# A patch-embedding tower on one core: early pair loads, earlier routing of the first groups, another opening, and the positions' squares folded into their table

## Time and profile before

| | us |
|---|---|
| timed runs (3) | 3396.25 to 3401.76, median 3399.97 |
| the profiled execution | 3385.79 |
| its span | 3383.9 |
| PE busy | 2483.1 (73%) |
| DVE busy | 2187.2 (65%) |
| ACT busy | 1658.6 (49%) |
| POOL busy | 2434.6 (72%) |

### The profile page before, as it was taken

How to read it: one execution, slowest core, us unless ns; L and a number is a source line. 1 busy time by engine, 2 the same in 40 slices (tenths; PEclk the granted TensorE clock), 3 DMA queues, 4 the chain that set the end, 5 groups by cost and what they waited for, 6 DMA issues and landing times. The chain is left out here.

```text
span 3383.9 us, 63281 instructions
## 1 busy us (share of the span) xinstructions
PE 2483.1 (73%) x14081; PEld 1880.2 (56%) x14082; DVE 2187.2 (65%) x7770; ACT 1658.6 (49%) x4362; POOL 2434.6 (72%) x2518
## 2 busy tenths in 40 slices
PE   5999995788777757666766377787787787777773
PEld 4877774454444434333433166676676676666663
DVE  5999997688876767767765444444444444577775
ACT  5988886556554545545543033333333333333332
POOL 4777772077777777777777777777777777777776
PEclk8999998567665676766665579878878878777886
DMA  8877872133333333333333154444444444699996
GB/s 304 285 262 264 268 266 102 35 98 105 104 104 95 101 96 96 100 96 99 98 97 96 63 135 128 128 126 114 112 113 112 111 112 113 212 303 302 303 303 214
DMA packets 401951, 522.41 MB, mean 154 GB/s; under 512 B 65661, under 2 KB 329555, under 8 KB 390579
## 3 DMA queue, kind: packets, MB, share of 16 engines
q1 hardware_dynamic: 318610, 373.60, 37.2%
q0 software_dynamic: 83232, 147.75, 12.9%
HBM read 257.02 MB, written 264.08 MB: 154 GB/s over the span
## 5 line engine op out<-in xcount | busy, mean ns | idle before, releaser
L1109 POOL DMA_INDIRECT ytk<-yo,idxy x1080 | 1055.8, 978 | 329.4 <-issue 324.2
L1100 POOL DMA_INDIRECT xed<-xr,idxs x1014 | 998.3, 985 | 392.0 <-issue 308.1
L1520 ACT ACTIVATE yo<-wide,gi 128x128 f32<-128x128 f32 x1080 | 307.8, 368 | 865.1 <-DMA ytk<-yo,idxy 836.5
L1372 PE MATMUL wide<-wdt,hT 64*128 x2160 | 376.0, 324 | 184.1 <-DVE hT L1877 181.1
L1868 DVE SCALAR_TENSOR_TENSOR ae<-the,bank 128x256 f32<-128x256 f32 x270 | 113.5, 420 | 604.1 <-ACT the L1511 590.9
L1354 PE MATMUL bank<-wgu,xeT 128*128 x2160 | 370.1, 325 | 140.8 <-ACT xeT L1505 138.1
L1372 PEld LDWEIGHTS wide<-wdt,hT 64*128 64x128 f32 x2160 | 316.9, 222 | 235.2 <-issue 232.1
L1354 PEld LDWEIGHTS bank<-wgu,xeT 128*128 128x128 f32 x2160 | 330.8, 234 | 182.2 <-issue 181.6
L594 POOL TENSOR_TENSOR weff<-w,gam 128x384 f32<-128x384 f32 x338 | 268.8, 830 | 10.1 <-DMA tokb<-in_tokb 8.7
L1282 PE MATMUL wide<-xn,e 128*128 128x128 f32 (+3 forms) x1024 | 274.2, 391 | 1.6 <-ACT e L1442 1.6
L1290 PE MATMUL wide<-ident,xr 128*128 128x128 f32 x169 | 44.6, 414 | 250.4 <-DVE xr L1613 250.4
(11 more groups left out here) (334 smaller groups left out, 5060.1 us busy)
## 6 DMA issues: line engine op xcount, KB each, us to landing
xin<-xed SPq DMA_DIRECT2D x1080, 74.0 KB
ytk<-zeros SPq DMA_DIRECT2D x42, 1536.0 KB, 9.6
yg<-ytk SPq DMA_DIRECT2D x42, 1536.0 KB, 7.9
xs<-in_xcol SPq DMA_DIRECT2D x42, 1280.0 KB, 6.7
ytk<-yo,idxy POOLq DMA_INDIRECT x1080
xed<-xr,idxs POOLq DMA_INDIRECT x1014
H<-in_ximg SPq DMA_DIRECT2D x4, 2704.0 KB, 22.1
h1d<-H SPq DMA_DIRECT2D x42, 256.0 KB, 9.5
```

The costliest lines, as they stand in the source:

```text
L1100: p.indirect_dma_start(xed[:, :], bass.IndirectOffsetOnAxis(ap=idxs[:, slot, j, k:k + 1], axis=0), xr[:, slot, j, :], None).then_inc(scat[ ...
L1109: p.indirect_dma_start(ytk[:, :], bass.IndirectOffsetOnAxis(ap=idxy[:, slot, j:j + 1], axis=0), yo[:, slot % ES, j, :], None)\
L1372: last = pe.matmul(eO[slot % 2][:, j * D:(j + 1) * D], hT[:, slot % 2, j, :], wdt[:, bass.ds(e, 1), :].rearrange("p o f -> p (o f)"), star ...
L1520: last = a.activation(yo[:, slot % ES, j, :], eO[slot % 2][:, j * D:(j + 1) * D], ACT.Copy, scale=gi[:, slot, j, 0:1])
```

## The change

It has four parts.

- `h1s` and the semaphores of its loads belong to the whole kernel. POOL clears it in the opening; SP loads the first two pairs at the end of the first stage, as soon as all h1 stores have landed, and the second stage doesn't load them or wait for the memset.
- `step_of` gives the first groups other steps: first halves at 3, 5, 6, 8 (before: 4, 6, 7, 9), second halves of the first three at 4, 6, 8 (before: 6, 7, 9). From the first half of group 4 and the second half of group 3 on, all is as before. SP's store of h4 has lag 2 instead of 3.
- In the opening ACT copies the row terms ahead of the second quarter of the images, not the fourth, and TensorE does `conv_x` of group 0 ahead of the positions' squares.
- The positions' squares are in the table itself: `post` becomes `sum_d(p^2 + 2 p) / D - 2 p`, and `xT` becomes x + 1. As a normalised x sums to 0 over d, the product is |p|^2 - 2 x.p. The splitting, three small DMAs, and the two bf16 products per group go; the squares are summed by two float32 products over all 128 partitions, and DVE combines them at the end of `statistics`. ACT's copy to `xT` is Identity with a bias of ones, where it was Copy.

```diff
+FIRST_HALF = {0: 3, 1: 5, 2: 6, 3: 8}
+SECOND_HALF = {0: 4, 1: 6, 2: 8}
+def step_of(g, lag, late):
+    if lag == 0:
+        return FIRST_HALF.get(g, place_of(g, late))
+    if lag == 1:
+        return SECOND_HALF.get(g, place_of(g + 1, late))
+    return place_of(g + lag, late)
...
+            elif isinstance(i, int):
+                for g in range(r_first, r_stop):
+                    if step_of(g, lag, late) == period * i + u:
+                        fn(g, g % 4, g // 4)
             elif third != 1:
-                g = 4 * i + (c - lag)
-                if not isinstance(g, int) or r_first <= g < r_stop:
-                    fn(g, (c - lag) % 4, i + (c - lag) // 4)
+                fn(4 * i + (c - lag), (c - lag) % 4, i + (c - lag) // 4)
...
+def load_pair(sp, h1d, h1s, h1_in, g, slot):
+    src = h1d[bass.ds(2 * g, 2), :, :].rearrange("b t d -> t b d")
+    sp.dma_start(h1s[:, slot, 0:4:2, :], src[0:HALF[0]]).then_inc(h1_in[slot], 16)
+    sp.dma_start(h1s[0:HALF[1], slot, 1:4:2, :], src[HALF[0]:T]).then_inc(h1_in[slot], 16)
...
-        def store_squares(sp):
...
+            g.memset(c["h1s"][:, :, :, :], 0.0).then_inc(s_zero, 1)
...
-        def split_squares(g):
...
+            v.wait_ge(s_psq, 3)
+            v.scalar_tensor_tensor(post[:, :], wide[1][:, 0:NN], 1.0 / D, post2[:, :], ALU.mult, ALU.subtract).then_inc(s_post, 1)
...
-                if i == 3:
+                if i == 1:
                     a.wait_ge(s_gb, 1)
...
-            a.activation(post[:, :], post[:, :], ACT.Copy, scale=-2.0).then_inc(s_psq, 1)
+            a.activation(post2[:, :], post[:, :], ACT.Copy, scale=2.0).then_inc(s_psq, 1)
...
-            pe.matmul(wide[1][0:1, 0:NN], ones[:, 0:1], possq[:, :], start=True, stop=True).then_inc(s_psq, 1)
+            pe.matmul(wide[1][:, 0:NN], ones[:, :], possq[:, :], start=True, stop=False)
+            pe.matmul(wide[1][:, 0:NN], ones[:, :], post2[:, :], start=False, stop=True).then_inc(s_psq, 1)
...
-                store_squares(sp)
...
-                sp.wait_ge(yt_zero, 16 * GA)
                 sp.wait_ge(h1_out[0], 16 * (-(-GA // 2)))
                 sp.wait_ge(h1_out[1], 16 * (GA // 2))
+                for g in range(2):
+                    load_pair(sp, h1d, c["h1s"], c["h1_in"], g, g)
+                sp.wait_ge(yt_zero, 16 * GA)
...
-                    pe.wait_ge(s_ps3, 48)
-                    nj = tiles_of(g)
-                    for j in range(0, nj, 2):
-                        m = min(2, nj - j)
-                        for i in range(j, j + m):
-                            pe.matmul(psD[:, i * NN:(i + 1) * NN], xT[:, i, :], post[:, :], start=(i == j), stop=False)
-                        last = pe.matmul(psD[:, j * NN:(j + m) * NN], onesb[0:3, :],
-                                         psq3[:, :].unsqueeze(1).to_broadcast([3, m, NN]), start=False, stop=True)
+                    pe.wait_ge(s_post, 1)
+                    for j in range(tiles_of(g)):
+                        last = pe.matmul(psD[:, j * NN:(j + 1) * NN], xT[:, j, :], post[:, :], start=True, stop=True)
...
-                position_squares(pe)
                 conv_x(0, 0, 0)
+                position_squares(pe)
...
-                    a.activation(xT[:, 0:nj, :].rearrange("p j d -> p (j d)"), psT[:, 0:nj * D], ACT.Copy).then_inc(xT_ready, 1)
+                    a.activation(xT[:, 0:nj, :].rearrange("p j d -> p (j d)"), psT[:, 0:nj * D], ACT.Identity,
+                                 bias=ones[:, 0:1]).then_inc(xT_ready, 1)
...
-            p.memset(h1s[:, :, :, :], 0.0).then_inc(n["s_h1"], 1)
...
-            sp.wait_ge(n["s_h1"], 1)
...
-            load_h1(0, 0, 0)
-            load_h1(1, 1, 0)
...
-                ('r', 3, halves(store_h4))], 0, GR)
+                ('r', 2, halves(store_h4))], 0, GR)
```

More of the change, by code:

```diff
@@ L202, in build @@
         mur = sb("mur", [128, B, 2, 2])
+        h1s = sb("h1s", [128, 2, 4, D])
+        h1_in = [sem(f"h1_in{i}") for i in range(2)]
         front(nc, io, sb, bank, wide, dict(
             ident=ident, identb=identb, ones=ones, onesb=onesb, before=before, beforeb=beforeb,
-            eps_ln=eps_ln, tenth=tenth, wq=wq, fscale=fscale, mur=mur), h1d, gbd, ytk)
+            eps_ln=eps_ln, tenth=tenth, wq=wq, fscale=fscale, mur=mur, h1s=h1s, h1_in=h1_in), h1d, gbd, ytk)
         back(nc, io, sb, sem, bank, wide, dict(
             ident=ident, identb=identb, ones=ones, onesb=onesb, before=before, beforeb=beforeb,
-            wq=wq, fscale=fscale, mur=mur, eps_ln=eps_ln), h1d, h3d, h4d, xed, ytk, out)
+            wq=wq, fscale=fscale, mur=mur, eps_ln=eps_ln, h1s=h1s, h1_in=h1_in), h1d, h3d, h4d, xed, ytk, out)
+def load_pair(sp, h1d, h1s, h1_in, g, slot):
+    src = h1d[bass.ds(2 * g, 2), :, :].rearrange("b t d -> t b d")
+    sp.dma_start(h1s[:, slot, 0:4:2, :], src[0:HALF[0]]).then_inc(h1_in[slot], 16)
+    sp.dma_start(h1s[0:HALF[1], slot, 1:4:2, :], src[HALF[0]:T]).then_inc(h1_in[slot], 16)
 def front(nc, io, sb0, bank, wide, c, h1d, gbd, ytk):
@@ L233, in front @@
         possq = sb("possq", [128, NN])
-        psqr = sb("psqr", [1, NN])
-        psq_parts = sb("psq_parts", [1, 3, NN], BF16)
-        psq3 = sb("psq3", [3, NN], BF16)
+        post2 = sb("post2", [128, NN])
         valt = sb("valt", [128, NN])
@@ L292, in front @@
         s_gpart = sem("s_gpart")
-        s_pq = sem("s_pq")
         s_const = sem("s_const")
@@ L305, in front @@
         s_psq = sem("s_psq")
-        s_psp = sem("s_psp")
-        s_ps3 = sem("s_ps3")
+        s_post = sem("s_post")
         s_v2 = sem("s_v2")
@@ L333, in store_rows @@
             sp.wait_ge(s_gbo, 96)
-        def store_squares(sp):
-            sp.wait_ge(s_psp, 5)
-            for k in range(3):
-                sp.dma_start(psq3[k:k + 1, :], psq_parts[:, k, :]).then_inc(s_ps3, 16)
         def constants(g):
@@ L608, in _ @@
                 split_rows(p)
-                split_squares(p)
                 fold(1, 1, 0)
@@ L676, in _ @@
                 mixed_values(pe)
+                conv_x(0, 0, 0)
                 position_squares(pe)
-                conv_x(0, 0, 0)
                 turn_moments(pe)
@@ L757, in _ @@
                 squares(a)
-                a.wait_ge(s_psq, 3)
-                a.activation(psqr[:, :], wide[1][0:1, 0:NN], ACT.Copy).then_inc(s_pq, 1)
                 a.wait_ge(s_mstd, 3)
@@ L879, in _ @@
                 v.wait_ge(s_mrT, 1)
-                v.wait_ge(s_zero, 2)
+                v.wait_ge(s_zero, 3)
                 mur = c["mur"]
@@ L968, in back @@
     uptob = sb("uptob", [128, 128], BF16)
-    h1s = sb_early("h1s", [128, 2, 4, D])
+    h1s, h1_in = c["h1s"], c["h1_in"]
     mrs = sb_early("mrs", [128, 2, 8])
@@ L1030, in back @@
     n = {}
-    for name in ("s_wt", "s_ws", "s_zr", "s_c", "upto_r", "s_c2", "s_h1",
+    for name in ("s_wt", "s_ws", "s_zr", "s_c", "upto_r", "s_c2",
                  "mrs_r", "xq_r", "q_r", "xqb_r", "qt_done", "xqT_r", "ffn_done", "h2_r", "bnc",
@@ L1041, in back @@
         n[name] = sem(name)
-    h1_in = [sem(f"h1_in{i}") for i in range(2)]
     h3_out = [sem(f"h3_out{i}") for i in range(2)]
@@ L1120, in load_h1 @@
                 after(sp, n["h2_r"], g - 1)
-                src = h1d[bass.ds(2 * g, 2), :, :].rearrange("b t d -> t b d")
-                sp.dma_start(h1s[:, slot, 0:4:2, :], src[0:HALF[0]]).then_inc(h1_in[slot], 16)
-                sp.dma_start(h1s[0:HALF[1], slot, 1:4:2, :], src[HALF[0]:T]).then_inc(h1_in[slot], 16)
+                load_pair(sp, h1d, h1s, h1_in, g, slot)
             def store_h3(g, slot, rnd):
```

2 lines of the change are left out of this document (1 added, 1 removed).

## The result

The kernel after took 3379.94 us (median of 6, 3377.11 to 3382.69), the kernel before on the same chip 3398.56 (6 runs): ratio 0.9939 (0.9929 to 0.9950), 18.6 us less. A copy of it, timed again on a second chip, took 3366.05 (5 runs) against 3384.50 (21): 0.9947 (0.9933 to 0.9960), 18.4 us less.

The account below looks back on a forecast made before the run. POOL's unbroken indirect DMAs from the first scatter on were taken to bound the end, DVE the first stage. Crossing -5.5, opening -4.5, squares -1.0 and routing -12.3 sum to -23.3: 3400.0 to 3376.7, so 3377 us, range 3360 to 3393.

Parts of the forecast that it names:

- rival C: The opening's stores land no sooner, or ACT starts late after the crossing: 3382 us; chance 0.14.
- The crossing: Between first and second stage: early loads let ACT start with the others at 581.5, -5.5 us, bounds 0 and -5.6.
- The opening: Start of the kernel: rows split sooner, conv_x(0) before the squares, conv_gb(0) near 49; -4.5 us, between 0 and -5.1.
- The squares: First stage: two bf16 matmuls fewer per group, gaining only in filling and draining; -1.0 us, bounds 0 and -31.
- Rival B: TensorE sets the pace of the first stage: a further -30 us, 3347; chance 0.08.
- The routing: Second stage: first groups routed sooner, 20.3 us at the first scatter, 8 lost as idle POOL; -12.3 us.
- my step 4, 5 and 6: DVE's steps in the second stage, in the clock of before: starting at 638.4, 655.0 and 675.9.
- The stall of a light step: Early routing: load waits for the store's round trip, 7.2 us after attn_out, all of it stalling DVE.
- The 8 us that POOL was to lose between groups: Routing: POOL idles about 8 us before groups 1 to 4, longest before group 1, and never later.
- Rival A: Stalls swallow the routing: each of four tight steps costs 3 us more, total -11, 3389; chance 0.13.
- POOL and its tail shift as a block: After the early scatters, POOL's indirect DMAs run back to back, so they and the tail move together.
- Rival D: ACT reloads its table around the new Identity in each first-stage group: slower by 40 to 90 us; chance 0.03.

## Why the prediction was right, and where it was not

The time was right (3377 forecast, 3379.94 measured), with one term wrong. The gain, though, is 18.6 us where 23.3 were forecast; the time is closer than the gain, as the median of the kernel before was 3399.97 at the time of the forecast and 3398.56 in this comparison. The measured gain lies nearer to rival C's 18 us than to my sum, and the first half of that rival is what happened.

*The crossing*: -5.5 forecast, -5.6 in this pair and -5.6 in the run of this part. ACT starts with the stage, as said; POOL's unexplained 8 us there touched nobody (rival C's second half).

*The opening*: -4.5 forecast, -0.1 measured. The failed step is "I take -4.5, between 0 and -5.1". That the stores begin at about 40 was right, and that they "have until 47.5" was the error: my own row gave 15 us from first issue to gbx, and I set 7.5 against it. From SP they are 13 us of slow small writes, from 39.1 to 52.2 us, whether issued at 26 or at 37. Rival C's first half came true; without this term the sum is -18.8. The first scatter, forecast at 645, came at 648.71 for the same reason. The Trainium skill's rule of ring order (DMA: Bandwidth & Descriptors, "Queues, rings and completion order"), by which the gain could be as low as 0, was on the right side: with one load less in front the stores started at 36.46. The ring set when they began, and their own rate did the rest.

*The squares*: -1.0 forecast, -0.9 in this pair. That agreement proves nothing: from the first `conv_gb` to the last h1 three traces with the squares' matmuls have 515.0, 515.9 and 513.9 us, the two of the kernel after 514.1 and 513.7. Rival B (TensorE sets the pace) fell: of the 29.2 us of matmuls that went, 9.8 came off TensorE's busy time, the rest went into slower matmuls at a lower granted clock, its wait for DVE grew by 8.7, and the stage all but kept its length.

*The routing*: -12.3 forecast; 14.1 in this pair, 11.4 in the other, 12.7 or 9.5 for the part alone against the two traces of before. The steps were worked out well: shifted by the 6.7 us of the front, my step 4, 5 and 6 should quantise at 631.7, 648.3 and 669.2, and did at 631.69, 648.79 and 669.81; the row of group 4 at 782.4 came at 780.66. The stall of a light step was forecast at 7.2 and took 7.11 and 7.74, by luck in its parts: the store took 3.9 us to come back, not 2.0, and the load 2.8, not 4.6. The 8 us that POOL was to lose between groups are 8.1, of which 6.41 before group 1. Rival A (stalls 3 us longer) fell.

*The sum at the end*: -20.8 and -19.2 at the 97th scatter, -18.6 and -18.4 in the medians. "POOL and its tail shift as a block" was nearly right for the medians. In the traces the block from the 97th scatter to the last spread took 2565.1 and 2565.0 us before, 2576.8 and 2566.5 after. That the medians come within 0.4 us of the sum without the opening is partly luck: the routing gave more than forecast in the first pair, and what the block took back behind it hid that.

*Rival D* fell: Identity brought no table load, as the Trainium skill had it (ScalarE: Activation LUTs, "Table sets: the hidden batching unit"); this trace now shows it for the set of the first stage.

## What to carry to other kernels

When one engine runs without a pause to the end, price a change at its first work and at the point from which it never waits again; the difference between the two is what the supply loses. A store that something waits for is priced from the moment at which what stands in front of it has drained, plus its own write time. Issuing it 11 us sooner behind the same loads moved nothing here, and another queue made it worse; one load less in front moved it by 2.6 us. And look for small instructions that take several times their usual length beside another engine's work: `xsq` at 535 ns instead of 146 cost this tuned kernel 12 us of its first stage.

## What the hardware showed that I had not expected

VectorE's small instructions with two SBUF operands take 0.15 to 0.16 us when POOL is idle, and 0.14 to 0.16 with one operand in PSUM even in the middle of a fold. Beside POOL's folds they wait, as a rule for the fold under way: in the kernel before 39 of the 43 `vr` end at a fold's end while the next fold follows at once. The first `vr` of the pipeline is the exception. It got in only when the whole chain had ended, after 7.65 us beside 24 folds and 1.58 beside 16, while the second got in after one fold of a chain of 8. Kernel before, POOL and DVE:

```profile
49.64 10.88 POOL L594 TENSOR_TENSOR weff<-w,gam 128x384 f32<-128x384 f32 x16
...
58.96 1.58 DVE L797 SCALAR_TENSOR_TENSOR vr<-mv,rs 128x4 f32<-128x4 f32 x1
...
61.87 5.47 POOL L594 TENSOR_TENSOR weff<-w,gam 128x384 f32<-128x384 f32 x8 [1.35 <-PE bank L633]
...
66.00 0.79 DVE L797 SCALAR_TENSOR_TENSOR vr<-mv,rs 128x4 f32<-128x4 f32 x1
```

What sets the first chain apart is not shown; in the kernel after, where the first `vr` meets a chain of 8, it takes 0.80. Whether the chain breaks hung on TensorE's `conv_gb(1)` (60.18 with the crossing alone, 61.41 in the kernel before), so a harmless edit elsewhere cost 4.2 to 5.3 us.

The other direction shows in the routing stage, POOL's timeline of the kernel after:

```profile
999.81 0.96 POOL L1100 DMA_INDIRECT xed<-xr,idxs  x1 [0.30 <-issue]
1001.08 1.34 POOL L1100 DMA_INDIRECT xed<-xr,idxs  x1 [0.31 <-issue]
1002.73 1.48 POOL L1100 DMA_INDIRECT xed<-xr,idxs  x1 [0.30 <-issue]
```

I matched the scatters that start from 1000 to 1300 us with the DVE instruction then under way. Of those that start under the quantising's first `tensor_tensor` (L1554, two SBUF operands), 10 of 11 took over 1.05 us; of 51 that start while DVE does nothing, none. In the other three traces of the two kernels it is 6 of 8, 6 of 11 and 6 of 11, and while DVE does nothing 1 of 175. What the scatters take beyond 0.96 us adds up, over the 917 from the 97th on, to 20.9 and 19.9 us before, 21.3 with the routing alone, 30.7 and 23.2 after. Less this, the five traces need 1159.1 to 1159.7 us for them, so stretched scatters are the whole difference of POOL's pace in that part. The Trainium skill (SBUF — State Buffer, "SBUF: two separate sides") has the rule that GpSimd cannot write descriptors while a VectorE operation in a two-port mode holds the shared ports; it does not name a `tensor_tensor` there. That the port is what stretches them is argued, not shown.
